# A vision tower with routed experts on one core: packs sent behind the rows, one exponential moved to POOL, registers loaded earlier, ACT's order turned, masks in pieces

## The reference, cut to what matters

```python
h = tok(x)                        # 16 images: 64 patches of 256 pixels each, two noisy linears, mish gate, W3, position
h = concat([cls_tok, h], 1)       # 65 tokens of 128 numbers per image
h = h + attn(layernorm(h))        # 8 heads, causal; scores normed by running mean and variance instead of a softmax
xf = layernorm(h)                 # then the mixture of experts on every token:
gate_vals, idx = top_k(xf @ router_w, 2)      # 8 experts, the best 2 of each token
gates = softmax(gate_vals)
for e in range(8):
    y = layernorm_e(xf + relu(xf @ w1[e] + b1[e]) @ w2[e] + b2[e]) * gamma[e] + beta[e]
    out += (gate of e for the token, or 0) * y
return h + out
```

## Time and profile before

| | |
|---|---|
| median of 3 runs | 156.25 us (155.98 to 159.85) |
| the profiled execution | 156.29 us |
| its span, first to last instruction | 154.5 us |
| PE, DVE, ACT, POOL busy | 80%, 71%, 46%, 41% of the span |
| chain that ended last | PE 39%, DVE 17%, issue 17%, DMA 10%, POOL 8% |
| largest gap of PE | 80.6 to 89.7 us, ahead of the first slot |

### The profile page before, as it was taken

The page is one execution under the profiler, slowest core; times in us unless marked ns, Lnnn a source line. Parts: engine busy times, 40 slices in busy tenths (PEclk is TensorE's granted clock), DMA queues, the critical chain, the costliest instruction groups (busy, mean ns, idle before and its releaser), DMA issues.

```text
span 154.5 us, 3855 instructions
## 1 busy us (share of the span) xinstructions
PE 123.7 (80%) x1144; PEld 110.0 (71%) x1144; DVE 109.4 (71%) x448; ACT 70.6 (46%) x205; POOL 62.6 (41%) x98
## 2 busy tenths in 40 slices
PE   7999678999999996376660079999989899999920
PEld 7946674898778894255550069999979899998920
DVE  1399999798767688585875031888979998887570
ACT  5437026453473540124140015787766878794000
POOL 8649500000000033771557230278666488772000
PEclk9999999999999999555555556999999999999995
DMA  5997799999930000111048916575959996012606
GB/s 129 301 450 305 291 387 396 346 293 296 281 117 2 4 6 0 52 52 35 20 102 231 356 51 215 162 192 161 317 146 266 315 352 237 25 34 77 243 5 138
DMA packets 16519, 28.53 MB, mean 185 GB/s; under 512 B 1873, under 2 KB 9958, under 8 KB 16372
## 3 DMA queue, kind: packets, MB, share of 16 engines
q1 hardware_dynamic: 14020, 25.56, 51.3%
q0 software_dynamic: 1184, 2.14, 4.1%
q10 hardware_dynamic: 1296, 0.60, 1.5%
HBM read 19.55 MB, written 12.16 MB: 205 GB/s over the span
## 4 chain that ended last, share of the span: by engine, by line
PE 39%; DVE 17%; issue 17%; DMA 10%; POOL 8%; ACT 4%; SPq 1%; POOLq 1%; ACTq 0%
PE ps L1463 9%; PE ps L1483 7%; POOL back L514 6%; DMA xg<-rows 4%; DMA noise_sb<-noise 4%; PE ps L1323 3%; DMA rows<-x2k,row_at 3%; PE ps L1291 3%; PE ps L1348 2%; PE ps L1333 2%; PE ps L1273 2%; POOL xgb L509 2%; PE ps L1455 1%; PE ps L1371 1%; PE ps L1361 1%
## 5 line engine op out<-in xcount | busy, mean ns | idle before, releaser
L1483 PE MATMUL ps<-w_all,hid 128*128 x184 | 25.2, 281 | 1.6 <-issue 0.9
L1483 PEld LDWEIGHTS ps<-w_all,hid 128*128 128x128 f32 x184 | 22.8, 195 | 2.6 <-issue 2.5
L514 POOL DMA_INDIRECT back<-kTm,xg x16 | 16.5, 1032 | 16.9 <-ACT kTm L697 11.8
L483 POOL DMA_INDIRECT rows<-x2k,row_at x16 | 15.9, 994 | 13.8 <-issue 13.8
L688 ACT ACTIVATE hid<-ps,D 128x128 f32<-128x128 f32 x48 | 13.6, 361 | 13.1 <-PE ps L1463 13.1
L1117 DVE COPY xgT<-ps 128x128 f32<-128x128 f32 x23 | 6.5, 288 | 14.0 <-PE ps L1455 11.7
L491 POOL TENSOR_TENSOR ex<-e_base,dlt 128x5 f32<-128x5 f32 x1 | 1.2, 1210 | 37.3 <-DVE dlt L949 37.3
L1455 PE MATMUL ps<-body_sb,xg 128*128 128x128 f32 x23 | 6.6, 296 | 9.1 <-DMA xg<-rows 9.1
L1463 PE MATMUL ps<-xgT,D 128*128 128x128 f32 x96 | 13.7, 289 | 0.2 <-DVE xgT L1117 0.2
L1463 PEld LDWEIGHTS ps<-xgT,D 128*128 128x128 f32 x96 | 12.5, 203 | 0.5 <-DVE xgT L1117 0.5
L688 ACT ACTIVATE hid<-ps,last_parts 128x128 f32<-128x128 f32 x44 | 12.5, 361 | 0.7 <-PE ps L1463 0.7
(11 more groups left out here) (240 smaller groups left out, 290.8 us busy)
## 6 DMA issues: line engine op xcount, KB each, us to landing
rows<-blank SPq DMA_DIRECT2D x8, 589.5 KB, 6.4
D<-pack SPq DMA_DIRECT2D x12, 386.0 KB
last_parts<-pack SPq DMA_DIRECT2D x11, 386.0 KB, 4.3
pack<-w1b SPq DMA_DIRECT2D x1, 2064.0 KB, 15.2
w_all<-w SPq DMA_DIRECT2D x1, 2048.0 KB, 12.0
xg<-rows SPq DMA_DIRECT2D x18, 65.5 KB, 3.1
back<-zeros SPq DMA_DIRECT2D x1, 1152.0 KB, 8.4
xT_oT<-patches SPq DMA_DIRECT2D x2, 512.0 KB, 5.7
```

The costliest lines, as they stand in the source:

```text
L483: nc.gpsimd.indirect_dma_start(rows, bass.IndirectOffsetOnAxis(ap=row_at[:, k, t:t + 1], axis=0), x2k[:, t, k, :], None, bounds_check=EXPE ...
L514: nc.gpsimd.indirect_dma_start(back, bass.IndirectOffsetOnAxis(ap=xg[j][:, P:P + 1].bitcast(U32), axis=0), z[j], None, bounds_check=P * K ...
L1483: last = mm(ps[:, 6 + j % 2, 0:P], hid[j % 2][:, f, :], w2_all[:, bass.ds(expert_j, 1), f, :].rearrange("p a n -> p (a n)"), start=(f == 0 ...
```

## The change

It has five parts.

1. **Packs and local rows.** Of the 5 early packs only the first is issued at once. The second waits for the 12 dispatches of parts 0 and 1, the third, fourth and fifth for the landing of the rows of slots 1, 3 and 4. The row loads of the 3 local slots move on SP from behind slots 6, 7, 8 to behind slots 10, 11, 12.
2. **POOL.** The exponentials of part 1 are taken on POOL as a power (two columns), behind part 0's dispatches, instead of on ACT. The biases of slots 0 and 1 are added between the dispatches of the last two tiles of part 2.
3. **Registers.** ACT loads the tile numbers of the early slots ahead of part 2's exponential; PE loads the early experts ahead of `rank(2)`.
4. **ACT's order in the slot loop** is units(j), deviation(j-2), scaled(j-2); it was deviation(j-2), units(j), scaled(j-2).
5. **Masks.** Each of the 3 masks (1152 columns) is built in 3 pieces of 384 columns, one in each of the iterations 10 to 18; it was a whole mask in the iterations 8, 11 and 14.

```diff
+PACK_BEHIND, LOCAL_AT = [1, 3, 4], 10
+PICK_FROM, PICK_PARTS = 10, 3
+PICK_W = NT * P // PICK_PARTS
...
             for j, expert_j in enumerate(early_values(mybir.EngineType.SP, early_expert, EXPERTS - 1)):
+                if j == 1:
+                    sp.wait_ge(dispatched, 16 * K * AHEAD_T)
+                if j >= 2:
+                    sp.wait_ge(xg_loaded[row_sem(PACK_BEHIND[j - 2])], 16)
                 sp.dma_start(packed[j], pack[:, bass.ds(expert_j, 1), :].rearrange("p a n -> p (a n)")
...
-                if EARLY + 1 <= j < EARLY + 1 + LOCAL:
-                    local = SENT + j - EARLY - 1
+                if LOCAL_AT <= j < LOCAL_AT + LOCAL:
+                    local = SENT + j - LOCAL_AT
...
+            power(0)
             dispatch(0, 0)
             dispatch(1, 0)
             dispatch(2, 0)
             dispatch(3, 0)
+            power(1)
             dispatch(CLS + 1, 1)
             dispatch(CLS + 2, 1)
-            dispatch(CLS + 3, 2)
-            dispatch(CLS + 4, 2)
-
-            pool.wait_ge(back_blank, 16)
...
-            for j in range(SLOTS):
+            dispatch(CLS + 3, 2)
+            with_bias(0)
+            with_bias(1)
+            dispatch(CLS + 4, 2)
+            pool.wait_ge(back_blank, 16)
+            for j in range(2, SLOTS):
                 with_bias(j)
-                if 2 <= j < SENT + 2:
+                if j < SENT + 2:
                     send(j - 2)
...
-            exp_gates(1)
             copy_norm2(2)
             twice(2)
+            act.wait_ge(early_done, 2)
+            early_tiles = early_values(mybir.EngineType.Activation, early_tile, EXPERTS * SEG)
             exp_gates(2)
...
             for j in range(SLOTS + 2):
-                if j >= 2:
-                    deviation(j - 2)
...
                 if j < SLOTS:
                     units(j)
                 if j >= 2:
+                    deviation(j - 2)
                     scaled(j - 2)
...
-                nc.vector.tensor_scalar(picks[n], token_cols, xg[j][:, P + 2:P + 3], None, ALU.is_equal).then_inc(picked, 1)
+                nc.vector.tensor_scalar(picks[n][:, cols], token_cols[:, cols], xg[j][:, P + 2:P + 3], None, ALU.is_equal
+                                        ).then_inc(picked, 1)
...
-                if j in PICK_AT:
-                    pick_rows(PICK_AT.index(j))
+                if PICK_FROM <= j < PICK_FROM + LOCAL * PICK_PARTS:
+                    pick_rows((j - PICK_FROM) // PICK_PARTS, (j - PICK_FROM) % PICK_PARTS)
...
             route(2)
+            pe.wait_ge(early_done, 1)
+            w2_experts = dict(enumerate(early_values(mybir.EngineType.PE, early_expert, EXPERTS - 1)))
             rank(2)
...
-            pe.wait_ge(early_done, 1)
-            w2_experts = dict(enumerate(early_values(mybir.EngineType.PE, early_expert, EXPERTS - 1)))
```

## The result

The changed kernel takes 160.77 us (median of 20 runs, 157.38 to 166.56); the kernel before, run beside it on the same chip, takes 157.91 us (20 runs, 154.78 to 161.32). The ratio is 1.0126 with a 95% interval of 1.0084 to 1.0167. Run again later beside other kernels, the change gave 159.85 us against 156.51, ratio 1.0202 (1.0118 to 1.0286). So it is slower by 2 to 3 us. The prediction was 154.3 us, 2 us less than before, in a range of 151.0 to 157.5.

The account below looks back on a forecast made before the run. It took SP's queue up to pack 13 as deciding: of the start's 4.4 us, slot 13's units keep 117.7 against 118.99, then 17.8 to slot 19's scaling, 135.5 against 137.49; gain 2.0, 156.29 to 154.3 us, range 151.0 to 157.5.

Parts of the forecast that it names:

- ACT's order: Slot loop on ACT: 2.01 us per iteration, 39.9 us from slot 2's units to slot 19's scaling against 40.1, even.
- SP's stretch: SP from row 5 to pack 13: 22.87 us as before, limiting slot 13 and cutting the start's gain of 4.4 us.
- Gates: Part 1's gates on DVE: the 0.94 us wait for ACT's exponential goes, last dispatch at 77.9 instead of 78.81.
- Landings: Start: part 1's last dispatch lands in 2.9 us (was 4.41), the rows in 4.2 (was 6.13); PE starts 4.4 earlier.
- Part 2's last dispatches: POOL, behind two biases: the last starts at 87.5 (was 84.81), lands in 3.5 us, row 5 at 91.0.
- The last dispatches come late: Rival, chance 0.13: rows land late, POOL's last dispatch starts at 91.0, row 5 follows after 93.0; 156.6 to 160.2 us.
- The slot that I read: ACT's row at 118.99 taken as slot 13's units before; forecast 117.7, then 17.8 us to slot 19's scaling.
- Masks: DVE in the slot loop: a third of a mask takes about 0.25 us, fits in 0.35 of slack, costs nothing.
- DVE and POOL collide: Rival, chance 0.05: nine mask pieces each wait for a POOL bias, six behind slot 13, costing 2.2 us; 156.5 us.
- Registers: Early register loads moved on PE ahead of `rank(2)` and on ACT: no effect, nothing.
- The clock: Rival, chance 0.13: PE's wait of 2 to 3 us at slots 12 and 13 halves its clock, 1.4 us more; 155.7 us.

Follow-up runs that it names:

- b_pp: Kernel before, with only part 1's power on POOL and the early packs held back; 156.41 us, ratio to before 0.9806.
- c_pph: Kernel before, with power on POOL, early packs held back, and four SP register groups loaded ahead of row 5; 158.06 us, ratio to before 0.9918.
- e_late: Kernel before, with power on POOL, packs held back, and part 2's last two dispatches behind the biases; 159.42 us, ratio to before 1.0001.
- c_hoist: Kernel before, with four of SP's eight register groups loaded before row 5; 158.15 us, ratio to before 0.995.
- d_mid3: Kernel before, with power on POOL, packs held back, and three SP register groups loaded between early packs 1 and 2; 153.94 us, ratio to before 0.9672.
- b_actnew: Kernel before, with ACT's new order alone; 163.53 us (before 158.54), no ratio given.
- e_act: Kernel before, with power on POOL, packs held back, and ACT's new order; 158.35 us, ratio to before 1.0013.
- a_both: Changed kernel, with part 2's last dispatches ahead of the biases again and ACT's old order; 159.55 us, ratio to before 0.986.
- a_dispfirst: Changed kernel, with both last tiles of part 2 dispatched ahead of the biases of slots 0 and 1; 159.62 us (before 158.54).
- g_best: Kernel before, with power on POOL, packs held back, three SP register groups between packs 1 and 2, masks in pieces, later local rows; 156.26 us, ratio 0.9872.
- f_reg: Kernel before, with power on POOL, packs held back, masks in pieces, later local rows, PE's early register load ahead of `rank(2)`; 156.17 us, ratio 0.9924.
- a_actold: Changed kernel, with ACT's old order (root, units, scaling); 162.78 us, ratio to before 1.0274.
- e_ml: Kernel before, with power on POOL, packs held back, masks in pieces and later local rows; 156.06 us, ratio to before 0.9907.

## Why the prediction was wrong

The sign was wrong. The step that failed is the one that I had called decisive, SP's, by the terms that feed it; and next to it the term of ACT's order.

Behind D, slot 19's scaling was forecast at 57.6 and came at 60.7, 3.1 us later. By the places, row 5 was 2.4 late (the dispatches 0.5, their landing 1.9). SP's stretch to pack 13 was 1.6 shorter than taken, pack 13 to its units took 4.6 instead of 3.8, and the stretch behind slot 13 took 19.4 instead of 17.8.

- **Gates**: the wait of 0.94 us went; part 1's gate operation follows `row_at` at once. From part 1's logits on DVE to D it is 11.03 to 11.14 us in the four profiles without the power on POOL and 9.36 to 10.40 in the 13 with it: 0.6 to 1.8 us gained, by most of them 1.6, where I took 0.9. The gain lies ahead of D and is not in the table.
- **Landings**: PE at 7.7 where I had 7.3, and the gain of the start right in size. Two errors cancel in part: ACT's row loads went out 3.9 us behind D (forecast 3.1), and from there to PE's transpose it was 3.8 us (forecast 4.2). The Trainium skill's rule (DMA: Bandwidth & Descriptors, Queues, rings and completion order), by which I had it that holding packs back would bring little, would have made this wrong; in b_pp, PE starts 3.3 us sooner behind D.
- **Part 2's last dispatches**: 10.1 against 9.6, nearly right. Their landing is what I mis-sized: 4.72 us on the chain where I took 3.5, and 5.4 from dispatch to row 5. Packs 2 to 4 go out at 95.68 to 96.84, right ahead of them. That these packs slow the landing is not shown: from the last dispatch to row 5 it is 4.7 to 6.4 us in all profiles but c_pph's. With the 0.5 us of the dispatches, row 5 was 2.4 us later than forecast. In the prediction's own terms that is 93.4, just past the 93.0 from which **"The last dispatches come late"** decides, and this rival is what happened: 156.6 us at its beginning, to which ACT's and the masks' share come. Its mechanism was only partly that; it had let the rows land late, and they did not. e_late shows the price alone: 4.4 us, of which up to 1.7 are the clock's.
- **SP's stretch**: 21.3 us against 22.87, so the limit was there, as the transfers and groups within it are. c_hoist and d_mid3 show that 2.7 to 4.8 us of what leads to pack 13 are register loads that fit elsewhere. I had left unsaid that row 14, behind pack 13, gates slot 13 too, by PE's order of transposes.
- **ACT's order**: the iteration of 2.01 was right (2.03), the comparison wrong. I set 19 iterations without any stall against 40.1 us of the old loop, stalls included. The loop keeps stalls with the new order as well (in b_actnew, slot 0's to slot 19's scaling takes 41.6 us, where 19 iterations of 2.03 make 38.6 and before takes 39.1), and what went was the old order's ability to run at 1.66 behind one. Shown by b_actnew (1.9 us) and e_act (2.2). In the full change it is hidden behind SP's waits up to slot 13 and counts behind it: there a_both takes 18.8 us where a_dispfirst, the same kernel with the new order, takes 20.1.
- **The slot that I read**: the row at 118.99 is slot 12's units (pack in `D`, an even slot), not slot 13's, which are these:

```profile
120.98 1.12 ACT L688 ACTIVATE hid<-ps,last_parts 128x128 f32<-128x128 f32 x4
```

  So before needs 16.5 us from there to slot 19's scaling, and my 17.8 for the change was already 1.3 slower than the kernel before; I took it for quicker. Had I counted right, the forecast's own sum would have shown ACT's cost.
- **Masks**: "about 0.25 us" for a third was 0.42, and DVE's slack of 0.35 does not hold it. Behind slot 13 the change took 19.4 us where its iteration alone gives 17.8; of these 1.6 us, e_act, with whole masks, has 0.9 as well (18.7). The rival "DVE and POOL collide" had 0.05 and a price of 2.2 us; g_best gives 1.6 for the pieces in all, the later local rows included. That POOL's work is what stretches DVE's instructions is read from ends that meet within 0.04 us; no run took POOL's work away. The Trainium skill (SBUF — State Buffer, SBUF: two separate sides) says that a POOL operation excludes a DVE operation in a two-port mode, and also one with two inputs in SBUF where POOL's reads SBUF too. The gain beside the bias is of the second kind and agrees (0.46 us for 0.16, ending 0.03 us behind the bias). The piece of 0.81 us in g_best agrees only in part: it ended 0.20 us behind the send beside it, sooner than a wait for the whole send with 0.42 us behind it.
- **Registers**: "nothing" was wrong for PE by 1.0 us at the last dispatch (f_reg), of which 0.1 reached row 5. In the change itself it is hidden, as the bias' wait for rows comes later than the ranks.
- **The clock** stayed at its full level, 2.4 GHz, behind the loop's first slots, through waits of 1.69 and 2.00 us (PEclk 1.00 in the change and in a_actold there). So that rival did not occur in the change, but it is no idle one: in e_late it did, behind a wait of 2.15.

What stays open: the terms don't add up to the measured times within 1 us. By the places, the change gains about 1.6 us ahead of D and loses 2.0 to 3.1 up to the load back; by the clock on the wall it is 2.0 to 3.3 slower. Other kernels miss to both sides: by the same reckoning b_pp should be 3.6 us faster and is 3.1, e_ml 3.8 and is 1.5, but e_late should be 0.8 slower and is level with before, and a_both should be 1.3 faster and is 2.2. D itself lies between 77.9 and 87.6 in the profiles, and between 78.8 and 83.9 in four kernels whose code ahead of it is the same. Whether the change has a hand in that I did not test.

## What to carry to other kernels

A loop's measured mean holds its stalls: compare a new order's free-running cycle with the old one's free-running cycle (here 2.03 with 1.66), never with the mean. Before an operation is put ahead of another on a queue, follow what waits behind it to the end: here two biases ahead of two dispatches cost 4.4 us at slot 19, the fall of the clock included, a register load ahead of the ranks moved a dispatch by 1.0, four register groups behind a new wait moved a row load by 4.7, while the same groups placed in a wait that was there anyway gained. And when a bundle is slower, take it apart: two of its parts gained 1.9%, and with one freed queue 2 to 3%.

## What the runs showed of the hardware

- A group of four register values on SP takes about 1.4 us (pack 5 follows row 5 after 1.90 with a group between them, after 0.51 without); four in a row took 6.46 us between two transfers (c_pph).
- An indirect transfer on POOL that lands in 2.3 us in a quiet stretch took 4.41 us beside five packs, 4.72 with three packs issued just ahead of it (the change), and 2.68 to 3.78 where one pack was issued ahead (b_pp, d_mid3, e_ml).
- The same comparison on DVE takes 0.82 us on 1152 columns and 0.42 on 384, once 0.81: cutting three masks into nine pieces makes 2.5 us into at least 3.8.
- In e_late PE had no work from about 100.1 to 102.2 us, and its granted clock was at the 1.2 GHz level from about 103.3 to 106.7, with PE busy, and then back at 2.4. No other profile shows such a fall in the loop.
